# Releasing the opening gathers of a recommendation network by counts of other engines' work

## The chip, the cores and the metric

The kernel runs on one core of a Trainium2 chip. The metric is the device time of one execution in microseconds (us), and less is better. Engines are named as in the profile: PE is the matmul engine (PEld its weight loads), DVE the vector engine, ACT the scalar engine, POOL the GpSimd engine, SP the engine that here only starts transfers. PEclk is the share of PE's full clock that was granted.

## What is computed

A batch of 2048 trips, each of 10 steps, goes through a small recommendation network:

```python
rp   = concat([region_tbl[region_idx], poi_tbl[poi_idx]], -1)          # (2048, 10, 12)
nv   = concat([rp @ W_rp + b_rp, coords @ W_co + b_co], -1)            # (2048, 10, 40)
conv = elu(conv1d(nv, conv_w, 3 taps, VALID) + conv_b)                 # (2048, 8, 32)
emb  = tanh(concat([car_tbl[car_idx], week_tbl[week_idx], time_tbl[time_idx]], -1))
x    = concat([conv, broadcast(emb)], -1)                              # (2048, 8, 59)
h    = lstm(lstm(x, layer 0), layer 1)                                 # H = 256, 8 steps
y    = ((h[:, -1] @ W1 + b1) @ W2 + b2) @ W3 + b3                      # (2048, 512)
```

All of it is in float32.

## The kernel before

The batch is cut into four parts of 512 trips, and a part lies in four groups of 128 trips, one for each row of 128 partitions (`GR` is 4). For a part, PE computes two LSTM layers over 8 steps; a "cell" is one layer at one step, 8 tiles of 128 gates by 512 trips (6 at step 0, which has no forget gate). The products use split float16 weights and states (`wh`, `h_part`), three products for one. Around the cells stand, once per part, the turning (transposing) of the features `feat`, the convolution, and the product of the turned embeddings `emb_in`.

Each engine runs its own program, written out by hand in order, and engines meet only at semaphores: an operation adds to one, and another engine waits for a count. What this case is about is the opening, the first 100 us, in which weights are loaded, turned and split and the first part is begun.

In the opening POOL fetches rows of tables with indirect transfers, one for each group and step: `gather_steps` fetches region rows for a step `t` in four gathers (the rows of the POI table come by products on PE in this first part), and `gather_emb` fetches the car and the time row of a group, two gathers for each `g`. The order on POOL is: steps 0 to 3 (16 gathers), the embeddings (8 gathers), `copy_emb` (two copies, of which the second, `L653`, lets PE turn the embeddings), steps 4 to 9 (24 gathers, with a wait for landing after every four), and later parts. The rows of even steps among the first four land on semaphore `rows_first_in[0]`, those of odd steps on `rows_first_in[1]`; a landed gather adds 16 (`DMA`).

PE's opening, in order: `product_w12` (`L1323`, the head's first two weight matrices multiplied together, eight pieces, each copied out by ACT at `L737`, which counts up `w12_put`), the band of the convolution, `turn_wx` (`L1348`, waits for `conv_band` of DVE), `turn_wh(0)` (`L1336`), the turning of steps 0 to 3 (`L1424`), more preparation (`L1411` is `product_head`), `turn_wh(1)`, then

```python
pe.wait_ge(emb_copied, 1)
turn_emb(acc[:, 0, :])
product_head(0, K2 // 2, K2)
first, second, *others = opening_cells(STEPS)
pe.wait_ge(emb_ready, 2)
```

then the first cell, a mix of embedding products (`L1458`) and `product_head`, the turning of steps 2 to 5, the second cell, `turn_wh(2)`, the third cell, the turning of steps 4 to 9, and the fourth. `emb_ready` comes from DVE (`split_emb`, `L1125`), which follows ACT's two tanh (`L780`, `L781`) of the turned embeddings. ACT does these after `put_wh_hi(1)`, four copies at `L743`.

Semaphores that the change names: `small_put` says that DVE has put the indices of the embeddings (`L928`), `poi_put` that the POI rows are in `feat` (`L1092`). `K2` is 8, `SIDES` is 2, `PAIR_WIN` is 4.

Of the kernel before, what the change touches and what calls it, by code (L numbers as in the profile page):

```python
# [19 lines left out]
DMA = 16  # L20
# [13 lines left out]
SIDES = 2  # L34
# [156 lines left out]
def build(nc, d):  # L191
# [17 lines left out]
    K1, K2, O = D1 // P, D2 // P, D3 // P  # L209
    STEPS = T - TAPS + 1  # L210
    NB = B // NCOL
    GR = NCOL // P
# [14 lines left out]
    with ExitStack() as ctx:  # L227
# [123 lines left out]
        rows_first_in = [sem("rows_even_in"), sem("rows_odd_in")]  # L351
# [6 lines left out]
        small_turned, small_put = sem("small_turned"), sem("small_put")  # L358
# [8 lines left out]
        poi_sum_step, poi_put = sem("poi_sum_step"), sem("poi_put")  # L367
# [13 lines left out]
        w12_acc, w12_put = sem("w12_acc"), sem("w12_put")  # L381
# [190 lines left out]
        @block.gpsimd  # L572
        def _(pool):
            nc.gpsimd.memset(ident[:, :], 0.0).then_inc(ident_zero, 1)
            pool.wait_ge(ident_zero, 1)
            nc.gpsimd.affine_select(out=ident[:, :], in_=ident[:, :], compare_op=ALU.not_equal, fill=1.0,
                                    base=0, pattern=[[-1, P]], channel_multiplier=1).then_inc(ident_ready, 1)
            pool.wait_ge(ident_ready, 1)
            for side in range(SIDES):
                if side:  # L580
                    pool.wait_ge(number_ready, side)
                nc.gpsimd.iota(poi_number[side * POI:(side + 1) * POI, :], pattern=[[0, 1]], base=0,
                               channel_multiplier=1, allow_small_or_imprecise_dtypes=True).then_inc(number_ready, 1)
            pool.wait_ge(number_ready, SIDES)

            nc.gpsimd.memset(poi_spread_f[:, :, :], 0.0).then_inc(poi_spread_step, 1)
            for side in range(SIDES):
                half = poi_spread_f[:, :, side * POI:(side + 1) * POI]
                pool.wait_ge(poi_spread_step, side + 1)
                nc.gpsimd.affine_select(out=half, in_=half, compare_op=ALU.not_equal, fill=1.0,  # L590
                                        base=-side * POI_PIECES, pattern=[[-1, POI_PIECES], [0, POI]],
                                        channel_multiplier=1).then_inc(poi_spread_step, 1)
            pool.wait_ge(poi_spread_step, 1 + SIDES)
            nc.gpsimd.tensor_copy(poi_spread[:, :, :], poi_spread_f[:, :, :]).then_inc(poi_spread_ready, 1)
            nc.gpsimd.iota(week_number[:, :], pattern=[[1, WEEK]], base=0, channel_multiplier=0,
                           allow_small_or_imprecise_dtypes=True).then_inc(week_number_ready, 1)
            nc.gpsimd.memset(proj_t[:, :], 0.0).then_inc(proj_t_zeroed, 1)
            nc.gpsimd.memset(poi_block[:, :, :, :], 0.0).then_inc(block_zeroed, 1)
            nc.gpsimd.memset(wx_rep[:, :, 3:7, D_EMB:Q], 0.0).then_inc(wx_copied, 1)
            nc.gpsimd.memset(emb[:, :, 0, D_EMB:Q], 0.0).then_inc(zeroed, 1)  # L600
            pool.wait_ge(zeroed, 1)

            def pace(n, cells):

                base = Base(n - 1, STEPS, plain)
                for layer, t in cells:
                    begin, tiles = (base.tile(t), 8) if t < STEPS else (Base(n, STEPS, plain).tile(t - STEPS),
                                                                        6 if t == STEPS else 8)
                    for k in range(tiles):
                        yield layer, begin + k + 1  # L610

            for n in range(NB):
                tiles = None

                def wait_tile():
                    if tiles is not None:
                        at = next(tiles, None)
                        if at is not None:
                            pool.wait_ge(gate_acc[at[0]], at[1])

                def gather(k, out, rows, landed):
                    wait_tile()
                    pool.indirect_dma_start(out, None, tables[k], bass.IndirectOffsetOnAxis(ap=rows, axis=0)  # L623
                                            ).then_inc(landed, DMA)

                def gather_steps(begin, end, poi, landed):
                    for t in range(begin, end):
                        for g in range(GR):
                            gather("region", feat[:, g, t, 0:D_REG], idx["region"][:, n * GR + g, t:t + 1], landed)
                            if poi:  # L630
                                gather("poi", feat[:, g, t, D_REG:D_REG + D_POI],
                                       idx["poi"][:, n * GR + g, t:t + 1], landed)

                def copy_coords():
                    nc.gpsimd.tensor_copy(feat[:, :, :, D_REG + D_POI:D_FEAT],  # L635
                                          coords[:, n * GR:(n + 1) * GR, :].rearrange("p g (t c) -> p g t c", c=2)
                                          ).then_inc(coords_put, 1)

                def gather_emb(begin, end):
                    for g in range(begin, end):  # L640
                        for k, at, cols in (("car", CAR_AT, slice(0, D_CAR)),
                                            ("time", TIME_AT, slice(D_CAR + D_WEEK, D_EMB))):
                            at += n * GR + g
                            gather(k, emb[:, g, 0, cols], small_idx[:, at:at + 1], emb_rows_in)

                def copy_emb():
                    if n == 0:
                        pool.wait_ge(week_put, 1)
                    nc.gpsimd.tensor_copy(emb[:, :, 0, D_CAR:D_CAR + D_WEEK], week_rows[:, n * GR:(n + 1) * GR, :]
                                          ).then_inc(week_copied, 1)  # L650
                    pool.wait_ge(week_copied, n + 1)
                    pool.wait_ge(emb_rows_in, (n + 1) * (2 * GR * DMA))
                    nc.gpsimd.tensor_copy(emb[:, :, 1:4, :],  # L653
                                          emb[:, :, 0, :].unsqueeze(2).to_broadcast([P, GR, 3, Q])
                                          ).then_inc(emb_copied, 1)

                if n == 0:

                    pool.wait_ge(idx_ready, 1)
                    for t in range(PAIR_WIN):  # L660
                        if t == PAIR_WIN // 2:
                            pool.wait_ge(rows_first_in[0], GR * DMA)
                            pool.wait_ge(rows_first_in[1], GR * DMA)
                        gather_steps(t, t + 1, False, rows_first_in[t % 2])
                    pool.wait_ge(small_put, 1)
                    for half in range(2):
                        pool.wait_ge(rows_first_in[half], 2 * GR * DMA)
                    gather_emb(0, GR)
                    copy_emb()
                    for t in range(PAIR_WIN, T):  # L670
                        landed = rows_in[0 if t < WIN else 1]
                        gather_steps(t, t + 1, False, landed)
                        pool.wait_ge(landed, (t - (PAIR_WIN if t < WIN else WIN) + 1) * GR * DMA)
                else:

                    for c in range(CH):
                        pool.wait_ge(turned[c], n)
                    if n == 1:
                        pool.wait_ge(later_coords_in, DMA)
                    copy_coords()  # L680
                    pool.wait_ge(emb_turned, n)
                    if n == 1:
                        pool.wait_ge(idx_ready, 3)
                    begun = list(pace(n, [(0, 3), (1, 2), (0, 4), (1, 3), (0, 5), (1, 4)]))
                    rows = GR * (2 + 2 * WIN)
                    tiles = (begun[i * len(begun) // rows] for i in range(rows))
                    gather_emb(0, GR)
                    gather_steps(0, WIN, True, rows_in[0])
                    tiles = None
                    copy_emb()  # L690
                    tiles = pace(n, [(1, 5), (0, 7), (1, 6), (0, 8)])
                    gather_steps(WIN, T, True, rows_in[1])
# [1033 lines left out]
```

## Time and profile before

| what | value |
|---|---|
| time, median of 3 runs | 1083.5 us (1082.26 to 1087.32) |
| time of the profiled execution | 1083.97 us |
| its span, first to last instruction | 1082.2 us |
| PE busy | 1060.1 us (98%) |
| DVE, ACT, POOL busy | 744.7, 516.6, 323.7 us |
| mean granted clock of PE | 0.997 |

The time of an execution is a little longer than the span of its trace, here by 1.8 us, which lies outside the traced instructions. A busy PE in the profile means that matmuls follow one another without a gap, and their ends are modelled. POOL's gathers count as busy for the time in which the engine makes up the transfer, not for the time until the rows are there.

### The profile page before, as it was taken

How to read it: one execution, taken by the hardware profiler on the slowest of the kernel's cores; microseconds unless marked ns; L12 is line 12 of the kernel's file. 1: busy time of each engine (PE TensorE's matmuls, PEld its weight loads, DVE VectorE, ACT ScalarE, POOL GpSimd, SP SyncE). 2: the span in 40 equal slices, each digit the busy share in tenths (PEclk: the TensorE clock that was granted, in tenths of full speed). 3: DMA queues.
4: the chain of work that ended last, by engine and by line, in shares of the span. 5: the costliest groups of instructions: out<-in, count | busy, mean ns of one | idle time of the engine just before them, and what ended most of it. 6: DMA issues, size and time to landing. Idle time of an engine off the chain costs nothing.

```text
span 1082.2 us, 14381 instructions
## 1 busy us (share of the span) xinstructions
PE 1060.1 (98%) x4905; PEld 508.2 (47%) x4905; DVE 744.7 (69%) x1162; ACT 516.6 (48%) x757; POOL 323.7 (30%) x340
## 2 busy tenths in 40 slices
PE   8799999999999999999999999999999999999998
PEld 6544444444445444444445444444444544444445
DVE  6688866665767866666867865567676775666554
ACT  3566344444555444434554544345554544444433
POOL 6551255624420056533440035552450000000000
PEclk9899999999999999999999999999999999999999
DMA  9410100000101100000011010000010110000001
GB/s 264 83 18 2 30 3 3 2 1 2 32 1 40 28 7 3 2 2 1 11 22 40 1 34 2 3 2 1 2 31 1 39 30 1 1 0 1 1 1 39
DMA packets 32082, 21.26 MB, mean 20 GB/s; under 512 B 19629, under 2 KB 25865, under 8 KB 32019
## 3 DMA queue, kind: packets, MB, share of 16 engines
q1 hardware_dynamic: 21223, 19.25, 6.1%
q0 software_dynamic: 9984, 1.12, 2.7%
q8 instruction: 38, 0.62, 0.2%
q14 instruction: 25, 0.20, 0.1%
q10 hardware_dynamic: 812, 0.07, 0.1%
HBM read 9.92 MB, written 4.19 MB: 13 GB/s over the span
## 4 chain that ended last, share of the span: by engine, by line
PE 87%; POOL 4%; DVE 3%; DMA 3%; issue 3%; ACT 0%; DVEq 0%; ACTq 0%; POOLq 0%
PE acc L1505 50%; PE acc L1496 27%; PE acc L1487 5%; POOL feat L623 3%; DMA feat<-in_L_rec_region_tbl,region_idx 2%; PE aux L1697 2%; PE acc L1530 1%; PE acc L1539 1%; POOL emb L623 1%; PE aux L1450 1%; PE aux L1444 0%; DVE head_sum L1029 0%; DMA region_raw<-in_r_region_idx 0%; DVE gates L1130 0%; DVE h_full L1177 0%
## 5 line engine op out<-in xcount | busy, mean ns | idle before, releaser
L1505 PE MATMUL acc<-h_part,wh 128*128 128x512 f16 (+1 forms) x2640 | 644.3, 380 | 0.0
L1505 PEld LDWEIGHTS acc<-h_part,wh 128*128 128x128 f16 x2640 | 240.2, 98 | 314.4 <-issue 55.1
L1496 PE MATMUL acc<-h_part,wh 128*128 128x512 f16 (+1 forms) x1440 | 346.9, 379 | 0.0
L803 ACT ACTIVATE gates<-acc,gate_bias,unscale 128x512 f32<-128x512 f32 x246 | 189.4, 777 | 299.8 <-PE acc L1505 261.1
L803 ACT ACTIVATE gates<-gates,gate_bias,unscale 128x512 f32<-128x512 f32 x242 | 188.9, 811 | 143.6 <-DVE gates L1130 133.3
L1496 PEld LDWEIGHTS acc<-h_part,wh 128*128 128x128 f16 x1440 | 139.9, 98 | 171.4 <-issue 6.2
L623 POOL DMA_INDIRECT feat<-in_L_rec_region_tbl,region_idx x160 | 162.6, 1016 | 168.8 <-PE acc L1505 126.2
L1130 DVE TENSOR_TENSOR gates<-acc,emb_gates 128x512 f32<-128x512 f32 x242 | 160.6, 686 | 45.4 <-PE acc L1505 33.0
L623 POOL DMA_INDIRECT feat<-in_L_rec_poi_tbl,poi_idx x120 | 120.6, 1005 | 111.0 <-PE acc L1505 93.1
L1487 PE MATMUL acc<-x_in,wx 96*128 96x512 f32 (+1 forms) x248 | 137.4, 560 | 2.9 <-DVE gates L1130 1.6
L1177 DVE TENSOR_TENSOR h_full<-gates,tanh_c 128x512 f32<-128x512 f32 x120 | 82.7, 689 | 75.3 <-ACT tanh_c L808 71.3
L1156 DVE TENSOR_TENSOR cell_c<-gates,cell_c 128x512 f32<-128x512 f32 x110 | 75.5, 686 | 73.8 <-ACT gates L803 70.0
L1151 DVE TENSOR_TENSOR ig<-gates 128x512 f32<-128x512 f32 x110 | 75.7, 688 | 62.5 <-ACT gates L803 58.8
L808 ACT ACTIVATE tanh_c<-cell_c 128x512 f32<-128x512 f32 x126 | 78.7, 625 | 65.3 <-DVE cell_c L1159 55.1
L1181 DVE TENSOR_TENSOR h_part<-h_full,h_part 128x512 f16<-128x512 f32 (+1 forms) x120 | 83.2, 693 | 16.1 <-DVE h_part L1178 5.6
L1159 DVE TENSOR_TENSOR cell_c<-cell_c,ig 128x512 f32<-128x512 f32 x110 | 76.2, 693 | 11.5
L1178 DVE TENSOR_TENSOR h_part<-gates,tanh_c 128x512 f16<-128x512 f32 (+1 forms) x120 | 83.1, 692 | 0.0
L1487 PEld LDWEIGHTS acc<-x_in,wx 96*128 96x128 f32 x248 | 47.1, 190 | 35.5 <-DVE gates L1130 5.3
L623 POOL DMA_INDIRECT emb<-in_L_rec_car_tbl,small_idx x16 | 16.5, 1034 | 119.7 <-PE acc L1505 111.3
L1103 DVE RECIPROCAL neg_part<-neg_part 128x512 f32<-128x512 f32 (+1 forms) x9 | 27.0, 2997 | 0.3
L635 POOL COPY feat<-coords 128x80 f32<-128x80 f32 x3 | 0.8, 254 | 80.2 <-PE aux L1424 80.2
L1697 PE MATMUL aux<-w_head,h_last 128*128 128x512 f32 x72 | 17.8, 403 | 0.0
(179 smaller groups left out, 411.8 us busy)
## 6 DMA issues: line engine op xcount, KB each, us to landing
out<-y SPq DMA_DIRECT2D x16, 256.0 KB, 2.1
x_in<-conv_hi SPq DMA_DIRECT2D x56, 64.0 KB
feat<-in_L_rec_region_tbl,region_idx POOLq DMA_INDIRECT x160
w<-in_L_rec_W SPq DMA_DIRECT2D x4, 512.0 KB, 5.3
w_nat<-in_L_rec_Whh SPq DMA_DIRECT2D x2, 1024.0 KB
w<-in_L_rec_W SPq DMA_DIRECT2D x1, 2048.0 KB
feat<-in_L_rec_poi_tbl,poi_idx POOLq DMA_INDIRECT x120
x_in<-conv_lo SPq DMA_DIRECT2D x28, 64.0 KB
```

Of the source, the lines that this page charges most:

```text
L623: pool.indirect_dma_start(out, None, tables[k], bass.IndirectOffsetOnAxis(ap=rows, axis=0)).then_inc(landed, DMA)
L803: nc.scalar.activation(gates[layer][:, j, g, :], source, ACT.Tanh if g == GATE_G else ACT.Sigmoid, bias=gate_bias[:, layer, m:m + 1], scal ...
L808: nc.scalar.activation(tanh_c[layer][:, j, :], cell_c[layer][:, j, :], ACT.Tanh).then_inc(tanh_c_done[layer], 1)
L1130: nc.vector.tensor_tensor(gates[0][:, j, g, :], acc[:, s.bank(j, g), :], emb_gates[:, g * HK + j, :], ALU.add).then_inc(gate_sum, 1)
L1151: nc.vector.tensor_tensor(ig[:, j, :], i_gate, g_gate, ALU.mult).then_inc(ig_done[layer], 1)
L1159: nc.vector.tensor_tensor(c, c, ig[:, j, :], ALU.add).then_inc(c_done[layer], 1)
L1177: nc.vector.tensor_tensor(h_full[:, j, :], o_gate, th, ALU.mult).then_inc(h_full_done[layer], 1)
L1178: nc.vector.tensor_tensor(hi, o_gate, th, ALU.mult).then_inc(h_hi_done[layer], 1)
L1181: nc.vector.tensor_tensor(lo, h_full[:, j, :], hi, ALU.subtract).then_inc(h_done[layer], 1)
L1487: mm = nc.tensor.matmul(bank, wx[:, rows], x_in[:, s.t, :], start=True, stop=s.first and not s.opening)
L1496: mm = nc.tensor.matmul(bank, wh[:, 1, a, c, rows], h_part[0][:, s.write_slot, b, c, :], start=(c == 0 and a == b == HI), stop=(s.first an ...
L1505: mm = nc.tensor.matmul(bank, wh[:, own_w, a, c, rows], h_part[layer][:, s.read_slot, b, c, :], start=False, stop=(c == HK - 1 and a == LO))
```

## The change

The waits that pace POOL's first gathers are set differently. Before, the third step's gathers waited until all eight gathers of the first two steps had landed, and the embeddings' gathers waited until all sixteen had. Now steps 2 and 3 each wait for the four gathers two steps back. Step 2 also waits for three copied pieces of the head product (`w12_put`) and for the embeddings' indices. The embeddings' gathers wait for all eight pieces and for the POI rows; the first half of them waits for the landing of the even steps, and the second half for that of the odd ones. No gather is added, removed or reordered.

```diff
                     for t in range(PAIR_WIN):
+                        if t >= 2:
+                            pool.wait_ge(rows_first_in[t % 2], GR * DMA)
                         if t == PAIR_WIN // 2:
-                            pool.wait_ge(rows_first_in[0], GR * DMA)
-                            pool.wait_ge(rows_first_in[1], GR * DMA)
+                            pool.wait_ge(w12_put, 3)
+                            pool.wait_ge(small_put, 1)
                         gather_steps(t, t + 1, False, rows_first_in[t % 2])
-                    pool.wait_ge(small_put, 1)
-                    for half in range(2):
-                        pool.wait_ge(rows_first_in[half], 2 * GR * DMA)
-                    gather_emb(0, GR)
+                    pool.wait_ge(w12_put, K2)
+                    pool.wait_ge(poi_put, SIDES)
+                    for g in range(0, GR, 2):
+                        pool.wait_ge(rows_first_in[g // 2], 2 * GR * DMA)
+                        gather_emb(g, g + 2)
                     copy_emb()
```

The first place is on POOL, from the ninth gather to the first ones of the embeddings. `rows_even_in` and `rows_odd_in` are the two semaphores of `rows_first_in`; a row with x7 stands for eight gathers together with the row ahead of it.

```order
-L623 DMA feat<-in_L_rec_region_tbl,region_idx 128x8 [waits rows_odd_in,rows_even_in]
-L623 DMA feat<-in_L_rec_region_tbl,region_idx 128x8 x7
-L623 DMA emb<-in_L_rec_car_tbl,small_idx 128x16 [waits rows_odd_in,rows_even_in,small_put]
+L623 DMA feat<-in_L_rec_region_tbl,region_idx 128x8 [waits small_put,w12_put,rows_even_in]
+L623 DMA feat<-in_L_rec_region_tbl,region_idx 128x8 x3
+L623 DMA feat<-in_L_rec_region_tbl,region_idx 128x8 [waits rows_odd_in]
+L623 DMA feat<-in_L_rec_region_tbl,region_idx 128x8 x3
+L623 DMA emb<-in_L_rec_car_tbl,small_idx 128x16 [waits rows_even_in,poi_put,w12_put]
```

The gathers stand where they stood, and only what each waits for has moved: one of the two landings, with counts of ACT's and DVE's work beside it.

The second place is on PE, around the turning of the embeddings, in the changed kernel; line numbers there are higher by three, and the rows are otherwise those of before.

```order
L1339 MATMUL acc<-ident,w_nat 128x128 [waits wh_lo_put]
L1339 MATMUL acc<-ident,w_nat 128x128 x3
L1434 MATMUL acc<-ident,emb 128x128 [waits emb_copied]
L1434 MATMUL acc<-ident,emb 128x128 x3
L1414 MATMUL aux<-w,w_t 128x512 [waits w12_put,w3_in]
L1414 MATMUL aux<-w,w_t 128x512 x3
L1490 MATMUL acc<-x_in,wx 128x512 [waits wh_lo_put,x0_put,bias_ready,emb_ready]
```

Nothing moved here: PE waits for POOL's copy at `emb_copied`, and a few matmuls later for DVE at `emb_ready`.

## Rows read from the trace of the kernel before

**Rows 1.** The profile's page: span, and busy time by engine.

```profile
span 1082.2 us, 14381 instructions
PE 1060.1 (98%) x4905; PEld 508.2 (47%) x4905; DVE 744.7 (69%) x1162; ACT 516.6 (48%) x757; POOL 323.7 (30%) x340
```

**Rows 2.** Waits over the whole span: who waited for whom, total, times, longest.

```profile
PE aux L1348 <- DVE conv_band L998: 5.5, 1, 5.5
...
```

**Rows 3.** Timeline of POOL: start, duration, what [idle before <-releaser].

```profile
10.64 1.19 POOL L623 DMA_INDIRECT feat<-in_L_rec_region_tbl,region_idx  x1 [0.31 <-issue]
...
15.88 0.95 POOL L623 DMA_INDIRECT feat<-in_L_rec_region_tbl,region_idx  x1 [0.30 <-issue]
19.65 0.95 POOL L623 DMA_INDIRECT feat<-in_L_rec_region_tbl,region_idx  x1 [2.82 <-DMA feat<-in_L_rec_region_tbl,region_idx]
...
34.48 0.95 POOL L623 DMA_INDIRECT emb<-in_L_rec_car_tbl,small_idx  x1 [5.13 <-DMA feat<-in_L_rec_region_tbl,region_idx]
...
45.76 0.51 POOL L653 COPY emb<-emb 128x384 f32<-128x384 f32 x1 [1.29 <-DMA emb<-in_L_rec_time_tbl,small_idx]
```

**Rows 4.** The chain that ended last: start, duration; DMA from issue to landing.

```profile
15.88 3.01 DMA feat<-in_L_rec_region_tbl,region_idx
...
28.40 5.29 DMA feat<-in_L_rec_region_tbl,region_idx
```

**Rows 5.** Timeline of ACT, copies of the head product, the split, one later row.

```profile
14.34 0.37 ACT L737 COPY w_t<-acc 128x257 f32<-128x257 f32 x1 [2.31 <-issue]
...
28.20 0.37 ACT L737 COPY w_t<-acc 128x257 f32<-128x257 f32 x1 [2.48 <-remote]
...
46.09 1.56 ACT L743 CAST wh<-aux 128x512 f16<-128x512 f32 x3 [3.03 <-PE acc L1336]
...
48.50 0.64 ACT L781 ACTIVATE emb_in<-acc 128x512 fp32r<-128x512 f32 x1
...
307.31 2.12 ACT L803 ACTIVATE gates<-acc,gate_bias,unscale 128x512 f32<-128x512 f32 x3 [2.48 <-remote]
```

**Rows 6.** Timeline of PE, 42 to 133 us.

```profile
42.13 0.60 PE L1336 MATMUL aux<-ident,w_nat 128*128 128x128 f32 x4
...
44.05 0.60 PE L1336 MATMUL acc<-ident,w_nat 128*128 128x128 f32 x4
46.32 0.66 PE L1431 MATMUL acc<-ident,emb 128*128 128x128 f32 x4 [1.68 <-POOL emb L653]
46.82 3.60 PE L1411 MATMUL aux<-w,w_t 128*128 128x512 f32 x8
50.70 0.50 PE L1487 MATMUL acc<-x_in,wx 96*128 96x512 f32 x1 [0.28 <-issue]
...
60.68 0.62 PE L1424 MATMUL acc<-ident,feat 128*56 128x128 f32 x4 [1.33 <-DMA feat<-in_L_rec_region_tbl,region_idx]
61.06 0.71 PE L1458 MATMUL aux<-emb_in,we 128*128 128x512 f32 x2
...
89.35 0.64 PE L1424 MATMUL aux<-ident,feat 128*84 128x128 f32 x4 [1.53 <-DMA feat<-in_L_rec_region_tbl,region_idx]
...
132.39 0.50 PE L1487 MATMUL acc<-x_in,wx 96*128 96x512 f32 x1 [1.14 <-DVE gates L1130]
```

**Rows 7.** Timeline of DVE, the splits and copies of the opening.

```profile
31.07 0.29 DVE L998 COPY conv_band<-aux 84x128 f32<-84x128 f32 x1 [2.83 <-remote]
...
49.24 1.40 DVE L1125 TENSOR_TENSOR emb_in<-emb_tanh,emb_in 32x512 fp32r<-32x512 f32 x2
...
59.59 1.28 DVE L1188 COPY emb_gates<-aux 128x512 f32<-128x512 f32 x2
...
100.81 0.69 DVE L1130 TENSOR_TENSOR gates<-acc,emb_gates 128x512 f32<-128x512 f32 x1 [0.18 <-PE acc L1505]
```

**Rows 8.** Stretches of 1 us: busy us by engine, PEclk, DMA share, GB/s.

```profile
29.00:30.00 1.00, 0.00 (x0) 0.00 (x0) 0.00 (x0) 0.00 (x0) 0.35 (x1) 0.50 1.08 330
...
35.00:36.00 1.00, 1.00 (x9) 1.00 (x8) 0.84 (x2) 0.73 (x2) 0.70 (x2) 0.74 0.12 12
```

## The prediction

> **What bounds the kernel now.** I began with the page [rows 1]: PE is busy for 1060.1 of 1082.2 us, so the change can win only from the 22 us in which PE stands still, or from what decides when the opening ends. I then read who waits for whom [rows 2] and the timelines of the opening engine by engine [rows 3, 5 to 7]. PE's idle time near the change is four waits. The first, 5.5 us for `conv_band` [rows 2], does not hang on POOL. The other three do: 1.68 us at 46.32 for the copy of the embeddings, 1.33 us at 60.68 and 1.53 us at 89.35 for the landing of region rows [rows 6]. They add up to 4.54 us. That is the most that an earlier POOL can give back, unless it changes something that it does not own. The reader is to see in each row which engine came last, and then to ask who would have come second.
>
> **The change, part by part.**
>
> POOL, third step. POOL starts a gather every 1.25 us (0.95 us of work and 0.30 us of issue, [rows 3]), and the eighth starts at 15.88 [rows 3]. The ninth starts at 19.65 now, after 2.82 us of idle. The new wait is for the first four gathers. The fourth of them starts at 10.64 [rows 3]. Landing takes 3.01 us from the start of a gather at 15.88 and 5.29 us from that at 28.40, when weights load [rows 4], so it is landed at 13.7 to 15.9, before the ninth's turn at 17.13. The third copy of the head product ends at 14.34 + 0.37 = 14.71 [rows 5], so the count adds nothing. The ninth gather starts at 17.13 and the sixteenth at 17.13 + 7 x 1.25 = 25.88 in place of 28.40: 2.5 us earlier. The odd step's wait at 22.1 is for rows that landed at 15.88 + 3.01 = 18.9. It costs nothing.
>
> POOL, embeddings. The first starts at 34.48 now, 0.79 us after the landing at 28.40 + 5.29 = 33.69. The new bound is the eighth copy, which ends at 28.20 + 0.37 = 28.57 [rows 5]. The even step's last gather starts at 20.88 and lands by 26.2 at 5.29 us, which is sooner. With the same 0.8 us to wake, the first starts at 29.4, so 5.1 us earlier. The odd step lands by 25.88 + 5.29 = 31.2, and POOL asks for it at 29.4 + 5.0 = 34.4. So the eight follow one another, and `L653` runs at 40.7 in place of 45.76 [rows 3]. Queued behind it are the 24 region gathers of steps 4 to 9, with the same waits as before, so they come 5.1 us earlier as well: the rows for the turning at 60.68 are there at about 55.6, those for 89.35 at 84.2.
>
> PE, first wait, 1.68 us. PE finishes its transposes at 44.65 [rows 6] and would no longer wait. But the first cell does not start behind PE's own work: `L1487` at 50.70 comes right after DVE's second split at 49.24 + 1.40 = 50.64 [rows 7]. That one follows ACT's second tanh, started at 48.50, and ACT comes to its tanh only after four copies that began at 46.09, after 3.03 us of idle [rows 5]. The profile puts this idle down to PE's transposes, but the copy needs only the first four, which started at 42.13 and took 0.60 us [rows 6]. What ACT waits for from 43.06 to 46.09 is not shown. Between nothing and the whole, I take nothing: ACT stands still for 2.48 us "remote" at 28.20 and again for 2.48 us at 307.31 in the middle of a stream in which PE had not stopped [rows 5], so ACT has halts of this length of its own, tied to its program. The upper end: ACT copies as soon as it can, the fourth at 45.2; the turned embeddings are there at 45.3, the two tanh take 1.1 us, DVE, with a subtract behind each copy and 1.40 us of splits, is ready at about 48.7, and PE, with its 0.5 + 3.6 us from 44.65 [rows 6], is ready at 48.75. The cell starts 1.9 us earlier.
>
> PE, second wait, 1.33 us. PE comes to the turning at 59.35. It then wants two embedding products, 0.38 us behind the start of the turning, and the second of them needs the fifth copy of DVE, which ends near 59.59 + 0.68 = 60.27 [rows 7]. So the second product starts at 60.3 in place of 61.3, and everything behind it comes 1.0 us earlier. DVE and ACT take the next steps from this (`w_head`, the second convolution), so they move along with it. This is the one firm term: 1.0 us.
>
> PE, third wait, 1.53 us. With rows at 84.2 and PE at 87.8 - 1.0 = 86.8, this wait goes. But the next event is DVE's: the fifth tile of the fourth cell needs DVE's sum of its first, and DVE comes to that from its own dense work, which moves by only the 1.0 us. Behind the fourth cell the chain runs over DVE, until PE takes over again at 132.39 after 1.14 us of idle [rows 6]. What DVE can take up of PE's earlier tiles is the time in which it waits for PE there, 0.18 us at 100.81 [rows 7]. I put down 0.2 us.
>
> The sum: 0 + 1.0 + 0.2 = 1.2 us. The profiled execution took 1083.97 us, 0.5 us above the median of 1083.5 that is compared. Its span would go from 1082.2 to about 1081.0, and the median to 1083.5 - 1.2 = **1082.3 us**. A measurement of this kernel can tell about 0.5%, 5.4 us, from no change, so this is within it.
>
> **A rule weighed.** The row at 46.09 shows ACT idle for 3.03 us with its input ready [rows 5], and the likeliest reading is that ACT waited for its own code. The Trainium skill, in Runtime: NRT & Kernel Launch (Instruction fetch mechanics), says that an engine's next code is fetched while the present runs and that this is mostly hidden in straight code, and costs where a branch is taken. There is no branch of ACT between 28 and 46 us, so by that page the halt is something else and could go; the sum would then be the 3.1 us of the first rival below. No run here shows which is right. The same skill, in SBUF — State Buffer (A bandwidth-pool intuition that's wrong, and the warning ahead of it), says that certain copies of DVE keep GpSimd from writing its descriptors. That would speak against gathers moved to 29 to 39 us, beside DVE's subtracts; the first gather of the embeddings, at 34.48 and so beside the same subtracts, took 0.95 us [rows 3], and the sum stays.
>
> **The rivals.**
>
> *ACT's halt goes with the wait (20%).* If the halt at 46.09 is tied to POOL or to PE standing still, the upper end holds: 1.9 + 1.0 + 0.2 = 3.1 us, 1080.4 us. For it: ACT's start at 46.09 falls within POOL's copy, 45.76 to 46.27. Against: no semaphore joins the two.
>
> *The idle before 31.5 goes too (8%).* DVE's "remote" idle of 2.83 us before `conv_band` at 31.07 [rows 7] and PE's 5.5 us behind it [rows 2] fall in the time in which the transfer engines are full, and PE's clock, at its lower level of 1.2 GHz from 29 on, comes back to 2.4 GHz in the slice from 35 to 36, at 35.5 by its mean of 0.74 [rows 8]. If the gathers, 2.5 us earlier, leave that stretch emptier, up to 5.5 us and half of the 4.0 us that PE worked there at half clock come back, 7.5 us, besides the 1.2: 1074.8 us. Against: those gathers are small beside 350 GB/s of weights [rows 8], which all remain.
>
> *The change doesn't do what it says (10%).* The released gathers could just land later in the stream of weights, or the eighth copy come later than 28.6, so that the embeddings still start near 34. Then nothing moves and the time stays at 1083.5 us. Against: the copy's bound needs 5 us of delay.
>
> *Slower, through the clock (7%).* In my forecast PE stands still from 48.75 to 50.70, 2.0 us in one piece, where before it had 1.68 us and then 0.28 us. The clock is at half in the slice from 29 to 30 [rows 8], after PE had stood still since 31.5 - 5.5 = 26.0 [rows 2]. It stood at full over the pause of 1.68 us. If it fell here, as it did there, PE would work at half for some 6.5 us (29 to 35.5) and lose 3.2 us: 1083.5 - 1.2 + 3.2 = 1085.5 us. It decides if the pause before the first cell is met by such a fall, and not otherwise.
>
> **How the numbers follow.** The forecast has 55%, with a range of its own from 1080.5 to 1084: its 1.2 us can lack the 0.2, or hold a part of ACT's halt, and the median of three runs moves by a microsecond or two. The range to hold 8 in 10 takes in the first and third rivals and the slower one with that scatter: 1078.5 to 1086.0. It leaves out the second rival. Faster by over 0.5% is below 1078.1 us: the second rival, and a lucky first one, 9%. Slower by over 0.5% is above 1088.9 us: the clock with something more, 5%. The rest, 86%, is within 0.5%.
>
> **What would show it right or wrong.** Right: POOL's ninth gather at about 17.1, the first embedding gather at about 29.4, `L653` near 40.7. PE's waits at the turnings of the embeddings and of both feature blocks are gone, ACT's copy still begins near 46 after 3 us of idle, the first cell still starts near 50.7, and PE waits there for DVE. The second product after the first turning starts 1.0 us earlier. At about 131 PE waits for DVE a little longer than the 1.1 us of now. Wrong: a first cell before 50, which is the first rival, a `conv_band` well before 31, which is the second, a PEclk under 1.00 after 36 us, which is the slower one, or embeddings that start after 33.

## The result, and the profile after

The changed kernel took 1092.72 us (median of 5 runs, 1092.26 to 1094.04) where the kernel before took 1083.5 (5 runs, 1082.26 to 1087.32): a ratio of 1.0082, with a 95% interval of 1.0069 to 1.0095. It is 9.2 us slower, outside the range of the prediction. The sign isn't the program's alone: on another chip, at another time, the same kernel was 5.6 us faster than the one before, and a near copy of it was 5.3 to 5.8 us faster on three chips.

The page of the changed kernel, span and busy time by engine, against [rows 1]:

```profile
span 1090.7 us, 14381 instructions
PE 1062.3 (97%) x4905; PEld 508.5 (47%) x4905; DVE 744.3 (68%) x1162; ACT 516.9 (47%) x757; POOL 320.6 (29%) x340
```

The span has grown by 8.5 us and PE's busy time by 2.2, so most of the loss, 6.3 us, is time in which PE stands still. The view of waits over the stretch from 5 to 60 us (who waited for whom: total, times, longest) says where:

```profile
ACT w_t L740 <- remote: 12.9, 2, 11.3
POOL emb L623 <- ACT w_t L740: 11.3, 1, 11.3
...
PE aux L1364 <- DVE poi_hot L1063: 10.1, 1, 10.1
```

The 5.5 us of [rows 2] are gone, and in their place stands a wait of 10.1 us ahead of another product. POOL waits just as long, but not for the same thing. "remote" is the label for a wait whose releaser the trace can't name. The timeline of POOL, to be read against [rows 3]:

```profile
17.10 0.94 POOL L623 DMA_INDIRECT feat<-in_L_rec_region_tbl,region_idx  x1 [0.30 <-issue]
...
25.85 0.95 POOL L623 DMA_INDIRECT feat<-in_L_rec_region_tbl,region_idx  x1 [0.30 <-issue]
38.15 0.94 POOL L623 DMA_INDIRECT emb<-in_L_rec_car_tbl,small_idx  x1 [11.34 <-ACT w_t L740]
...
52.19 0.51 POOL L653 COPY emb<-emb 128x384 f32<-128x384 f32 x1
```

The sixteen gathers run as predicted, the ninth at 17.10 and the last at 25.85. But the embeddings come at 38.15, 3.7 us later than before: POOL stands for 11.34 us for the eighth copy of ACT. The timeline of ACT, against [rows 5], shows what held that copy:

```profile
14.78 0.37 ACT L740 COPY w_t<-acc 128x257 f32<-128x257 f32 x1 [2.31 <-issue]
26.46 0.37 ACT L740 COPY w_t<-acc 128x257 f32<-128x257 f32 x1 [11.31 <-remote]
...
37.50 0.37 ACT L740 COPY w_t<-acc 128x257 f32<-128x257 f32 x1 [1.37 <-PE acc L1326]
```

and the timelines of DVE (one row) and PE show the rest, against [rows 7] and [rows 6]:

```profile
29.32 1.41 DVE L1063 TENSOR_SCALAR poi_hot<-aux,poi_number 128x512 bf16<-128x512 f32 x2 [10.42 <-remote]
```

```profile
12.74 3.75 PE L1326 MATMUL acc<-w_t,w 128*128 128x257 f32 x16
16.42 0.60 PE L1393 MATMUL aux<-poi_row,poi_spread 10*128 10x512 bf16 x2
...
30.79 0.47 PE L1364 MATMUL aux<-ident,proj_nat 65*121 65x65 f32 x1 [10.10 <-DVE poi_hot L1063]
...
38.49 1.93 PE L1351 MATMUL aux<-ident,wx_rep 128*96 128x128 f32 x16 [0.27 <-DVE conv_band L1001]
...
47.36 1.12 PE L1441 MATMUL aux<-feat_t,conv_band 56*64 56x256 f32 x4 [3.41 <-issue]
48.40 5.67 PE L1414 MATMUL aux<-w,w_t 128*128 128x512 f32 x8
...
60.52 0.47 PE L1490 MATMUL acc<-x_in,wx 96*128 96x512 f32 x1 [0.83 <-DMA x_in<-conv_lo]
...
68.94 0.60 PE L1427 MATMUL acc<-ident,feat 128*56 128x128 f32 x4
...
96.51 0.60 PE L1427 MATMUL aux<-ident,feat 128*84 128x128 f32 x4
...
141.15 0.49 PE L1490 MATMUL acc<-x_in,wx 96*128 96x512 f32 x1 [1.14 <-DVE gates L1133]
```

Read the three engines together. PE ends the product for ACT's fourth copy by 16.5 and the two for `poi_hot` by 17.02. ACT begins the copy at 26.46, 10 us later, and DVE begins `poi_hot` at 29.32, 10.42 us after its last work. Both had nothing else to do. PE then waits for DVE's `poi_hot`, and the three engines stand still together. What is late is not PE's work but its count as ACT and DVE see it; when ACT and DVE do work, PE and POOL see their counts within a few tenths of a microsecond. In the trace of the kernel before, the same fourth copy came within 0.7 us of its product, which PE had ended by 16.05:

```profile
16.73 0.37 ACT L737 COPY w_t<-acc 128x257 f32<-128x257 f32 x1 [2.02 <-issue]
```

That the counts are held, and not the two engines, is a reading of these rows; no run isolates it. One rival can be looked up, that ACT and DVE waited for their own code. The view of transfers shows none of instructions between 5 and 31 us in this trace. The first two come at 32.5 and 33.1 us, when both engines have begun again.

Behind this the whole opening is late. The first cell starts at 60.52, 9.8 us after the 50.70 of [rows 6], and 141.15 answers to 132.39 there, 8.8 us later. PE's second halt, 3.41 us ahead of 47.36, is of the same kind. It waits for ACT's copy of `feat_t`:

```profile
46.73 0.58 ACT L762 COPY feat_t<-acc 56x512 f32<-56x512 f32 x1 [0.86 <-remote]
```

PE had turned `feat` by 42.77, but ACT stood still for 2.26 us ahead of the copy before this one and for 0.86 us ahead of this one.

The second part of the loss is the clock. In stretches of 1 us (busy by engine, PEclk, DMA share, GB/s):

```profile
48.00:49.00 1.00, 1.00 (x5) 0.50 (x2) 0.00 (x0) 0.12 (x1) 0.00 (x0) 0.50 0.12 6
...
52.00:53.00 1.00, 1.00 (x3) 0.51 (x2) 0.96 (x2) 1.00 (x3) 0.80 (x3) 0.80 0.00 0
```

After PE's idle 3.41 us ahead of 47.36 its granted clock is at the lower level (1.2 of 2.4 GHz), and comes back in the slice from 52 to 53, at 52.4 by its mean of 0.80. The first eight products of `product_head` take 5.67 us. The same eight took 3.70 in the kernel before:

```profile
38.60 3.70 PE L1411 MATMUL aux<-w,w_t 128*128 128x512 f32 x8
```

### The profile page after: what moved, and what is told of

It reads as the page before. It is cut to its first block, busy times and chain, and to the rows that moved or that the text cites. A ratio compares the mean times of both kernels' runs of the same rounds, so it can differ in the third digit from the quotient of the medians.

```text
span 1090.7 us, 14381 instructions
## 1 busy us (share of the span) xinstructions
PE 1062.3 (97%) x4905; PEld 508.5 (47%) x4905; DVE 744.3 (68%) x1162; ACT 516.9 (47%) x757; POOL 320.6 (29%) x340
## 4 chain that ended last, share of the span: by engine, by line
PE 87%; DVE 5%; issue 4%; SPq 3%; ACT 1%; DMA 0%; DVEq 0%; ACTq 0%
PE acc L1508 50%; PE acc L1499 27%; PE acc L1490 5%; SPq L495 3%; PE aux L1700 2%; PE acc L1533 1%; PE acc L1542 1%; DVE gates L1133 1%; ACT gates L806 1%; PE aux L1453 1%; DVE h_full L1180 1%; DVE h_part L1181 1%; PE aux L1447 0%; PE aux L1414 0%; DVE head_sum L1032 0%
## 5 line engine op out<-in xcount | busy, mean ns | idle before, releaser
L806 ACT ACTIVATE gates<-acc,gate_bias,unscale 128x512 f32<-128x512 f32 x246 | 189.4, 777 | 299.7 <-PE acc L1508 260.1
L806 ACT ACTIVATE gates<-gates,gate_bias,unscale 128x512 f32<-128x512 f32 x242 | 188.7, 811 | 143.5 <-DVE gates L1133 127.2
```

What stands on the lines that cost most here:

```text
L806: nc.scalar.activation(gates[layer][:, j, g, :], source, ACT.Tanh if g == GATE_G else ACT.Sigmoid, bias=gate_bias[:, layer, m:m + 1], scal ...
```

## The experiments

Each group of runs was made on one chip, beside the kernel before. The chips differ, so I name them: chip B, chip C (twice) and chip D, and chip A for the group with three copies of the changed kernel. Chip A was used at one time only, and which chip gave the result above isn't recorded.

**The parts apart (chip B).** The first theories were that a run of sixteen gathers without a halt brings the late counts, and that the hold on the pieces of the head product is too early or too late.

`e1_run16_old_emb`: the changed kernel with the embeddings' waits as before.

```diff
-pool.wait_ge(w12_put, K2)
-pool.wait_ge(poi_put, SIDES)
-for g in range(0, GR, 2):
-    pool.wait_ge(rows_first_in[g // 2], 2 * GR * DMA)
-    gather_emb(g, g + 2)
+pool.wait_ge(small_put, 1)
+for half in range(2):
+    pool.wait_ge(rows_first_in[half], 2 * GR * DMA)
+gather_emb(0, GR)
```

> Sixteen gathers in one run as in the changed kernel, the embeddings released by landing as in the kernel before (no count of the head product's eight pieces). Theory A, the run: once POOL has made about eight gathers without a pause, what PE counts up reaches ACT and DVE late until POOL stops. Then ACT's fourth copy of the head product (L740 in the changed kernel) comes at 26 to 27 us after 11 us of idle as in the changed kernel, DVE's fourth comparison near 29, and the time stays at 1088 to 1094 us. Theory B, the count: the loss comes of POOL being held from 26.8 to 38 us by the eight pieces. Then the time falls back to 1080 to 1085 us, and ACT's copy comes near 17.

`e2_run8_new_emb`: the opposite; the kernel before with this one block as changed.

> Steps 0 to 3 in two runs of eight with the landing wait between, as before; only the embeddings' gathers are released as in the changed kernel (eight pieces of the head product, POI rows, each half by its landing). Theory A: the run is back to eight, ACT's fourth copy of the head product comes near 17 and the time is within 3 us of before, 1080 to 1086 us. Theory B: POOL is held by the eight pieces, and the time is near that of the changed kernel, 1089 to 1093 us.

`e3_fours`: the kernel before, with a wait for landing after every four gathers, the embeddings' too.

```diff
-if t == PAIR_WIN // 2:
-    pool.wait_ge(rows_first_in[0], GR * DMA)
-    pool.wait_ge(rows_first_in[1], GR * DMA)
+if t:
+    pool.wait_ge(rows_first_in[(t - 1) % 2], ((t - 1) // 2 + 1) * GR * DMA)
...
-gather_emb(0, GR)
+gather_emb(0, GR // 2)
+pool.wait_ge(emb_rows_in, GR * DMA)
+gather_emb(GR // 2, GR)
```

> The kernel before with a landing wait after every four gathers, the embeddings' included. Theory A: no run is longer than four, so PE's counts are never late: ACT's eighth copy of the head product comes near 25.5 instead of 28.20, conv_band near 28.5 or earlier instead of 31.07, ACT's idle of 3.0 us before the copy at 46.09 is gone, and the clock of PE does not fall before the turning of wx. POOL pays three more landings of 2 to 4 us, so its embeddings copy comes at 50 to 54 us, which PE then waits for: the time is 1079 to 1087 us, set by POOL. Theory C, the load: the late counts between 22 and 31 us come of the weights' stream alone, then conv_band stays at 31 and the time is 1086 to 1091 us.

`e4_count5`: the changed kernel with another count.

```diff
-pool.wait_ge(w12_put, 3)
+pool.wait_ge(w12_put, 5)
```

> The changed kernel with five copied pieces of the head product in place of three as the release of the ninth gather: the count is reached near 19 us, so POOL pauses for some 2.5 us between the runs of eight, without a wait for all eight landings. Theory A with a pause enough: ACT's copies go on at 16.7, 18.6 and 20.5 as before and the time is 1080 to 1086 us. If it is the landing and not the pause that counts, the time stays at 1089 to 1093 us.

| chip B, before 1084.94 us | median us | ratio, 95% interval |
|---|---|---|
| e1_run16_old_emb | 1080.55 | 0.9963, 0.9949 to 0.9977 |
| e2_run8_new_emb | 1080.00 | 0.9952, 0.9936 to 0.9969 |
| e3_fours | 1092.78 | 1.0073, 1.0057 to 1.0090 |
| e4_count5 | 1079.25 | 0.9947, 0.9930 to 0.9963 |

Either part alone is faster, and on this chip the run of sixteen does not bring late counts: the trace of e1 has no "remote" row in its opening. This tells less than it seems to, for a chip without late counts can't say which part brings them. Only the fours are slower, and more so than the 1079 to 1087 us that were expected, for an everyday reason. Their timeline (POOL and PE together) shows it:

```profile
34.83 0.94 POOL L623 DMA_INDIRECT feat<-in_L_rec_region_tbl,region_idx  x1 [2.88 <-DMA feat<-in_L_rec_region_tbl,region_idx]
40.98 1.03 PE L1425 MATMUL acc<-ident,feat 128*56 128x128 f32 x4 [7.78 <-issue]
...
54.63 0.51 POOL L653 COPY emb<-emb 128x384 f32<-128x384 f32 x1 [1.39 <-DMA emb<-in_L_rec_time_tbl,small_idx]
55.19 0.95 PE L1432 MATMUL acc<-ident,emb 128*128 128x128 f32 x4 [3.44 <-POOL emb L653]
```

The gathers of the fourth step are issued only from 34.83 on (four at 1.25 us, the last at 38.58), so PE stands for 7.78 us before it can turn `feat` at 40.98, and for another 3.44 us before the embeddings. This slow opening costs 7.8 us by late gathers, nearly as much as the 9.2 by late counts. Only the releasers tell the two apart.

**Both kernels unchanged, and the holds (chip C).** All of this spoke for a faster kernel, so the two kernels themselves were run again.

> The kernel before, unchanged, with a profile from the same chip as the others of this group. Theory A (a long run of gathers delays PE's counts) has fallen with the sixteen in a run that were faster than before. What is open is whether the late counts belong to a kernel or to a single loading of it. Theory D, the kernel: the profile shows again ACT's eighth copy of the head product near 28.2, conv_band near 31.1 and ACT's idle of 3 us before 46.1, and the time is 1083 to 1086 us. Theory E, the loading: these places differ from the first profile by over 2 us, and the time stands off by as much.

> The changed kernel, unchanged. Theory D: ACT's fourth copy of the head product comes again near 26.5 after 11 us of idle, and the time is 1091 to 1094 us. Theory E: the copy comes elsewhere, near 16.5 if undisturbed, and the time then is 1078 to 1085 us.

`v1_no_w12_hold` leaves out the hold for all eight pieces, and `v2_count2` asks for two pieces where the change asks for three.

```diff
-pool.wait_ge(w12_put, K2)
```

> The changed kernel without the wait for all eight pieces ahead of the embeddings' gathers; the count of three and the POI rows stay. Theory D with this wait as its cause: near 1079 to 1082 us and no late counts, as in the run of sixteen with the old release of the embeddings. Theory D with the release of the ninth gather as its cause: 1089 to 1094 us and ACT's fourth copy near 26.

```diff
-pool.wait_ge(w12_put, 3)
+pool.wait_ge(w12_put, 2)
```

> The changed kernel with a count of two in place of three at the ninth gather, both long reached when POOL asks. Theory D: nothing changes, 1091 to 1094 us, with ACT's fourth copy near 26.5. Theory E or one in which the exact moment decides: a time off by over 5 us from the changed kernel's.

| chip C, before 1084.68 us | median us | ratio, 95% interval |
|---|---|---|
| r_before | 1084.09 | 0.9997, 0.9987 to 1.0007 |
| r_after | 1078.49 | 0.9946, 0.9929 to 0.9962 |
| v1_no_w12_hold | 1078.63 | 0.9947, 0.9930 to 0.9963 |
| v2_count2 | 1078.20 | 0.9944, 0.9927 to 0.9960 |

The change is faster here by 5.6 us, and the counts of pieces are without effect: two, three or five, with or without the eight. The kernel before, on this chip, by its timelines of PE and ACT:

```profile
47.74 0.60 ACT L780 ACTIVATE emb_tanh<-acc 128x512 f32<-128x512 f32 x1 [5.42 <-PE acc L1431]
...
40.99 0.60 PE L1336 MATMUL acc<-ident,w_nat 128*128 128x128 f32 x4
46.59 1.11 PE L1431 MATMUL acc<-ident,emb 128*128 128x128 f32 x4 [5.00 <-POOL emb L653]
47.50 5.07 PE L1411 MATMUL aux<-w,w_t 128*128 128x512 f32 x8
52.00 0.79 PE L1487 MATMUL acc<-x_in,wx 96*128 96x512 f32 x1
```

and the changed kernel, rows of ACT, DVE, PE and POOL:

```profile
15.94 0.37 ACT L740 COPY w_t<-acc 128x257 f32<-128x257 f32 x1 [1.37 <-PE acc L1326]
...
25.25 0.37 ACT L740 COPY w_t<-acc 128x257 f32<-128x257 f32 x1 [1.37 <-PE acc L1326]
...
18.69 1.41 DVE L1063 TENSOR_SCALAR poi_hot<-aux,poi_number 128x512 bf16<-128x512 f32 x2
...
20.16 0.32 PE L1364 MATMUL aux<-ident,proj_nat 65*121 65x65 f32 x1
...
41.42 0.60 PE L1339 MATMUL acc<-ident,w_nat 128*128 128x128 f32 x4
41.86 0.60 PE L1434 MATMUL acc<-ident,emb 128*128 128x128 f32 x4
42.30 3.60 PE L1414 MATMUL aux<-w,w_t 128*128 128x512 f32 x8
46.75 0.47 PE L1490 MATMUL acc<-x_in,wx 96*128 96x512 f32 x1 [0.86 <-DMA x_in<-conv_lo]
...
28.26 0.94 POOL L623 DMA_INDIRECT emb<-in_L_rec_car_tbl,small_idx  x1 [1.84 <-DMA feat<-in_L_rec_region_tbl,region_idx]
```

ACT's fourth copy begins at 15.94 here and at 26.46 above, DVE's `poi_hot` at 18.69 and at 29.32, PE's `L1364` at 20.16 and at 30.79: all three 10.5 or 10.6 us apart, in the same program. The gain on this chip can be added up at the first cell, which starts 5.25 us earlier (52.00 to 46.75). From PE's last transposes to the turning of the embeddings there were 46.59 - 40.99 = 5.60 us and are 0.44, a gain of 5.16. From the turning to the cell there were 5.41 us and are 4.89, although 0.86 of these is a new wait for the transfer of `conv_lo`. So the work itself took 5.41 and takes 4.03, a gain of 1.38: after its wait of 5.00 us PE ran at half clock, and after none it doesn't. PE gets to the transposes 0.43 us later than before. In sum 5.16 + 1.38 - 0.86 - 0.43 = 5.25.

**The loading or the chip (chip A).** Three copies of the changed kernel, each loaded anew, asked whether the late counts come with a loading of the program, so now in one copy and not in the next.

> The changed kernel, unchanged, loaded anew, to see how often its slow form comes. Theory E, the loading: each loading has its own form, so among three some may stand near 1092 us with late copies on ACT and DVE, and others near 1078.5 us. Theory F, a state that was there only in the first measurement: all three stand at 1077 to 1081 us, with ACT's fourth copy of the head product near 16.2.

> As the loading before this one: 1077 to 1081 us by theory F, and either form by theory E.

> As the two loadings before this one: 1077 to 1081 us by theory F, and either form by theory E.

They took 1091.38, 1089.62 and 1092.97 us, one execution each, and the kernel before beside them 1082.97. All three had late counts, and in none do instructions arrive by transfer before 29.3 us, when ACT and DVE have begun again. The first one's rows of ACT, DVE and PE:

```profile
25.18 0.37 ACT L740 COPY w_t<-acc 128x257 f32<-128x257 f32 x1 [10.38 <-remote]
...
27.36 0.75 DVE L1063 TENSOR_SCALAR poi_hot<-aux,poi_number 128x512 bf16<-128x512 f32 x1 [8.70 <-remote]
...
30.19 0.47 PE L1364 MATMUL aux<-ident,proj_nat 65*121 65x65 f32 x1 [9.85 <-DVE poi_hot L1063]
```

So it doesn't look drawn anew at each loading: all three loadings here had it, and none of the 15 loadings, of all kernels together, on chips B, C and D. It stays with the chip, or with the hour, and no run tells these two apart. A second mark goes with it. The view of one line, `L806` (the gates' activations in the cells, behind the opening), lists for the first copy what ended ACT's idle time there (us, times):

```profile
  remote: 7.3, 3
```

The given trace of the kernel before has the same 7.3 us in 3 pieces at its `L803`, one of them the 2.48 us at 307.31 in [rows 5], and that of the changed kernel 7.6 in 3. None of the 15 traces from chips B, C and D has such a row. So there are chips, or hours, in which ACT is now and then late to see PE's count, in both kernels, and others in which it isn't. Below, "a chip like A" stands for either.

**Once more, for such a chip (chips D and C).** The kernels that tell the theories apart on a chip like A ran twice more, with one in which sixteen gathers follow one another in a quiet stretch, from 140 to 162 us, in the second part.

> The sixteen in a run with the embeddings released by landing, once more. The changed kernel takes 1078.5 us on one chip and 1090 to 1093 us on another, where what PE counts up reaches ACT and DVE up to 11 us late from the ninth gather on. Theory G, chip and run: on a chip of the second kind the long run of gathers brings this on by itself. Then this kernel stands at 1088 to 1094 us there with ACT's fourth copy of the head product at 22 to 27 us; on a chip of the first kind it stays at 1080 to 1081 us. Theory H, chip and hold: the wait for the eight pieces is needed too, and this kernel stays near 1080 us on either.

> Two runs of eight with the landing wait between, and the embeddings released by counts. Theory G: as the count of five, 1079 to 1084 us on a chip of the second kind, 1080 us on one of the first.

> The changed kernel with a count of five, so a pause of some 2.5 us between two runs of eight. Theory G: on a chip of the second kind the late counts shrink to those of the kernel before (1 to 3 us between 22 and 31 us), and the time is 1079 to 1084 us. If the pause is of no use there, it stands at 1089 to 1093 us. On a chip of the first kind 1079 us again.

```diff
-tiles = (begun[i * len(begun) // rows] for i in range(rows))
+tiles = (None if n == 1 and 8 < i < 24 else begun[i * len(begun) // rows] for i in range(rows))
```

> The kernel before, with sixteen gathers in a run near 140 us, where before each waited for its own tile of PE; nothing else loads there. Theory G without any load: on a chip of the second kind PE's counts come late there too, PE loses 5 to 12 us and the time is 1088 to 1096 us. If the weights' stream is needed as well, nothing changes, 1083 to 1085 us. On a chip of the first kind 1084 to 1085 us.

> Eight gathers in a row with their count, the embeddings released as in the kernel before. If this chip is of the kind on which the counts of PE come 7 to 12 us late: by the theory that a run of 16 gathers right behind one another brings the delay, this one has it too, the fourth copy of the head product starts near 25 and the time is near 1092; by the theory that only the earlier embeddings bring it, 1080 to 1083. If no late counts are seen in the traces of this call, all three kernels are 3 to 6 us under the kernel before, and this is the third of such results (1080.6 and 1081.4 so far).

> The landing wait after the eighth gather kept as before, only the embeddings released by the counts. On a chip with late counts: by the theory of the run of 16, no delay, 1079 to 1083, since the halt of 2.8 us behind the eighth gather is kept; by the theory of the embeddings, near 1092. On a chip without: 1078.8 to 1080.

> The changed kernel with the ninth gather held for the fifth copied piece in place of the third. On a chip with late counts: the fifth copy itself comes after the fourth, so if the delay needs gathers under way it cannot arise before them and the time is 1079 to 1083; if the delay arises anyway, near 1092. On a chip without: near 1079.3.

| kernel | chip D, before 1084.56 us | chip C, before 1084.51 us |
|---|---|---|
| sixteen in a run, old embeddings | 1081.41; 0.9967, 0.9956 to 0.9979 | 1080.40; 0.9965, 0.9952 to 0.9977 |
| eights, new embeddings | 1078.78; 0.9948, 0.9932 to 0.9965 | 1079.11; 0.9949, 0.9933 to 0.9966 |
| count of five | 1079.28; 0.9949, 0.9933 to 0.9966 | 1078.70; 0.9948, 0.9932 to 0.9965 |
| sixteen in a run, later | 1085.08; 1.0005, 0.9995 to 1.0015 | |

Neither group met late counts, so neither tells which part of the change brings them on a chip like A. What they do settle is the split on the others, now on three chips: the early embeddings alone give 4.9 to 5.8 us, the run of sixteen alone 3.2 to 4.4, and together 5.3 to 6.2. The gains don't add, because both shorten the same wait. In the last trace with sixteen in a run and the old waits, the rows of PE and POOL are

```profile
44.05 0.66 PE L1433 MATMUL acc<-ident,emb 128*128 128x128 f32 x4 [3.01 <-POOL emb L653]
44.54 3.60 PE L1413 MATMUL aux<-w,w_t 128*128 128x512 f32 x8
...
32.11 0.94 POOL L623 DMA_INDIRECT emb<-in_L_rec_car_tbl,small_idx  x1 [5.65 <-DMA feat<-in_L_rec_region_tbl,region_idx]
```

so 3.01 us of the 5.00 are left, and the clock has held over this pause: the eight products take 3.60. It didn't hold in the same program's trace on chip D, whose first cell starts at 50.62 where this one's starts at 47.58:

```profile
44.16 1.11 PE L1433 MATMUL acc<-ident,emb 128*128 128x128 f32 x4 [3.06 <-POOL emb L653]
45.06 6.12 PE L1413 MATMUL aux<-w,w_t 128*128 128x512 f32 x8
```

## Why the prediction was wrong, point by point

- **Gathers 9 to 16.** Right: 17.10 and 25.85, predicted 17.13 and 25.88.
- **The embeddings at 29.4, and PE's own way: the step that failed.** The sentence was "the new bound is the eighth copy, which ends at 28.20 + 0.37 = 28.57 [rows 5]". It took ACT's copies from the trace before as fixed, and with them PE's opening ("PE finishes its transposes at 44.65"), while the change put eight gathers beside them without the halt at 16 to 19 us. On the measuring chip the eighth copy ended at 37.87, and PE came to the turning of the embeddings at 55.66. The rival "the change doesn't do what it says" named this very event ("or the eighth copy come later than 28.6") and priced it at nothing, as if only POOL would be late. But DVE's counts were late as well, and PE waited for DVE: at 30.79 it had stood still for 10.10 us. The late embeddings by themselves cost PE nothing, for at 55.66 it doesn't wait. POOL's two copies, at 51.93 and 52.19, were held by DVE's `week_rows` and not by the gathers, the last of which had been made up by 47.84:

```profile
51.93 0.19 POOL L649 COPY emb<-week_rows 128x12 f32<-128x12 f32 x1 [4.09 <-DVE week_rows L948]
```

The prediction left this bound out. In the trace before, `week_rows` ends at 40.99, so `L653` could not have run at 40.7.

- **Where the 9.8 us at the first cell come from.** PE's turning of the weights, which waited until 31.5 for `conv_band` [rows 2], starts at 38.49, 7.0 us later. From there to the first cell PE takes 22.03 us in place of 19.20, which is the other 2.8. Three things are added: the halt of 3.41 us, 2.0 us by which the eight products of `product_head` are longer, and a wait of 0.83 us for `conv_lo`. Two are saved: the 1.68 us for the embeddings, and 1.7 us at the turning of the weights, which runs at full clock (1.93 us) where it ran at half before:

```profile
31.50 3.62 PE L1348 MATMUL aux<-ident,wx_rep 128*96 128x128 f32 x16 [5.47 <-DVE conv_band L998]
```

- **PE's first wait, worth nothing.** On chip C it was worth 5.25 us. Two readings of [rows 5, 6] were wrong for it. PE reached the turning at 44.65 there but at 41.59 on chip C, so the wait was 1.68 and is 5.00. And ACT's halt at 46.09 was taken to be tied to its program, "halts of this length of its own". The same program on chip C has no such halt: `emb_tanh` runs as soon as PE has turned. The first rival was nearer (the halt can go), but its 3.1 us came from a trace in which the late counts already hid the size of the wait. To the kernel before they cost nothing here: its first cell starts at 50.70 with them and at 52.00 on chip C without.
- **The rule that was weighed.** The Trainium skill, in Runtime: NRT & Kernel Launch (Instruction fetch mechanics), made code an unlikely cause of the halt. The measurement agrees with it: the same instructions on chip C ran without the halt, and the trace before shows no transfer of instructions between 40 and 52 us, around the halt from 43.06 to 46.09. I had decided against the rule, from one trace.
- **The second and third waits, 1.0 and 0.2 us.** Right in kind and size. Both turnings, at 68.94 and 96.51, have no idle time ahead of them, and of the 9.82 us of delay at the first cell 8.85 are left at the eight products behind the first turning (70.46 for 61.61), and 8.76 at 141.15, a gain of 1.06.
- **Slower, through the clock.** The mechanism was there, at another pause: 3.41 us of idle, then half clock to 52.4, at a price of 2.0 us on the eight products where 3.2 was estimated.
- **The idle before 31.5.** On chip C it is shorter in the kernel before as well (PE waits 2.64 us for `conv_band`), so the length seen before went with the chip or the hour. Moving the gathers did not shorten it there: the changed kernel waits 3.36.

What stays open: on a chip like A, whether the run of sixteen alone, the early embeddings, or the two together bring counts that are 6 to 11 us late, where the kernel before has halts of 2.5 to 3; whether a count of five or the old halt after eight would cure it; what in the machine holds the counts; and whether it goes with the chip or with the hour. No run separates these. The first count that comes late is due at 16.5, just ahead of the ninth gather at 17.10, and in the kernel before POOL stands still from 16.8 to 19.65. This fits the run as the trigger, but it is only argued.

## What to carry to other kernels

A wait that is released by another engine's count ties this engine to that one's delays, so price it by what holds the counting engine, and price a late count for every engine that reads it. Before a halt in one trace is called a property of the program, look at the same program on another chip and at another time: here the same two kernels gave 9.2 us lost in one place and 5.6 won in another. When a wait on the path is removed, look at the clock in the stretch behind it: on chip C PE worked at half after 5.00 us of idle, and a quarter of the gain at the first cell was the clock's.

## What the runs showed of the hardware

- In all four traces of the changed kernel with late counts (the result's, and the three on chip A), ACT stood still for 7.40 to 11.31 us ahead of its fourth copy, and DVE for 5.83 to 10.42 us ahead of `poi_hot`, though PE had ended their products by 16.5 and 17.02. On chip C the same program had none, nor had its near copies on B and D. Waits in the other direction ended sooner. In the result's trace PE ran 0.06 us after DVE's `poi_hot`, and POOL 0.28 us after ACT's eighth copy.
- SP's issues slow down with it, though its rows name no wait. These two stand 1.39 us apart in the changed kernel on the measuring chip, and 0.34 us on chip C:

```profile
20.78 0.71 SPq L495 DMA_DIRECT2D bias_nat<-in_L_rec_b  x1
22.17 0.71 SPq L495 DMA_DIRECT2D w<-in_L_rec_W  x1
```

- The gathers themselves don't: POOL keeps 0.94 and 0.30 us through the whole stretch, so the busy engine looks sound while those around it stand still.
- The length of a pause alone doesn't decide what becomes of PE's clock. Ahead of the turning of the embeddings, one and the same program had a pause of 3.01 us on chip C and of 3.06 us on chip D. The clock stayed at its upper level behind the one (eight products in 3.60 us) and stood at 0.50 behind the other (6.12 us).
